# Attention sums spread one half a burst, turned two bursts later, with one bank wait per exp tile

## What is computed

```python
q, k = (x @ Wq) * scaling, x @ Wk          # 32 half-heads of 4 channels
v = x @ Wv                                  # 16 heads of 8 channels
probs = softmax(where(causal, q k^T, -inf))
attn = (probs[0::2] - lam * probs[1::2]) @ v
attn = attn * rsqrt(mean(attn^2) + eps) * rms_w * (1 - LAMBDA_INIT)
x = layernorm(x + attn @ Wo)
r, kk = sigmoid(xr @ W_r.T), square(relu(xk @ W_k.T))   # xr, xk mix x with the token before
x = layernorm(x + r * (kk @ W_v.T))
```

## Time and profile before

| | us |
|---|---|
| median of 3 runs | 507.17 (504.01 to 508.28) |
| profiled execution, device time | 505.25 |
| its span, first to last instruction | 503.5 |
| around the span | 1.75 |
| mean granted TensorE clock | 0.891 |

### The profile page before, as it was taken

How to read it: one execution, slowest core, us unless ns; L and a number is a source line. 1 busy time by engine, 2 the same in 40 slices (tenths; PEclk the granted TensorE clock), 3 DMA queues, 4 the chain that set the end, 5 groups by cost and what they waited for, 6 DMA issues and landing times.

```text
span 503.5 us, 14453 instructions
## 1 busy us (share of the span) xinstructions
PE 418.9 (83%) x5191; PEld 178.7 (35%) x5191; DVE 391.2 (78%) x504; ACT 354.7 (70%) x687; POOL 198.2 (39%) x349
## 2 busy tenths in 40 slices
PE   5665788898989898989898989889898978788682
PEld 3431323233434333333333333334242423344352
DVE  2769889797979999979797979898979894324633
ACT  3620168687878888968797969897969687756343
POOL 7000021253535364535354535545444445351512
PEclk9875569798979999979898979999989899989978
DMA  7695202011111120202020202020202010000001
GB/s 204 187 296 227 86 0 69 20 44 44 48 40 44 44 85 0 85 0 85 0 85 0 85 0 85 0 85 0 85 0 85 0 44 4 1 1 22 2 21 42
DMA packets 21082, 28.35 MB, mean 56 GB/s; under 512 B 3776, under 2 KB 8768, under 8 KB 21056
## 3 DMA queue, kind: packets, MB, share of 16 engines
q1 hardware_dynamic: 20624, 27.80, 17.5%
q10 hardware_dynamic: 432, 0.20, 0.2%
HBM read 18.29 MB, written 9.44 MB: 55 GB/s over the span
## 4 chain that ended last, share of the span: by engine, by line
PE 68%; ACT 15%; DVE 8%; issue 6%; DMA 1%; POOL 1%; ACTq 0%; POOLq 0%; DVEq 0%
PE acc L593 28%; PE ex L562 17%; ACT e_buf L898 11%; PE mx L516 7%; PE mx L508 6%; DVE part_max L989 5%; PE mx L690 1%; PE ex L624 1%; ACT o_tok L828 1%; PE ex L629 1%; PE mx L691 1%; DMA x_tok<-in_L_attn_x 1%; PE mx L675 1%; PE mx L710 1%; DVE rest L949 1%
## 5 line engine op out<-in xcount | busy, mean ns | idle before, releaser
L989 DVE TENSOR_REDUCE part_max<-mx 128x2 f32<-128x1024 f32 (+2 forms) x288 | 337.6, 1219 | 45.9 <-PE mx L508 35.8
L898 ACT ACTIVATE e_buf<-ex 128x512 f32<-128x512 f32 x576 | 312.1, 597 | 85.4 <-PE ex L562 81.0
L593 PE MATMUL acc<-e_buf,v_grp 128*32 128x256 f32 (+2 forms) x2200 | 185.5, 424 | 0.0
L562 PE MATMUL ex<-qe,ke 32*128 32x512 bf16 (+3 forms) x768 | 119.0, 346 | 44.0 <-ACT e_buf L898 29.2
L435 POOL TENSOR_SCALAR_AFFINE_SELECT e_buf<-e_buf 128x512 f32<-128x512 f32 x128 | 78.9, 634 | 169.5 <-ACT e_buf L898 169.4
L508 PE MATMUL mx<-km,qm 32*128 32x128 bf16 (+2 forms) x1280 | 124.4, 284 | 13.6 <-DVE part_max L989 12.1
L562 PEld LDWEIGHTS ex<-qe,ke 32*128 32x128 bf16 x768 | 30.9, 92 | 168.1 <-ACT e_buf L898 159.1
L593 PEld LDWEIGHTS acc<-e_buf,v_grp 128*32 128x32 f32 x2200 | 50.1, 115 | 65.6 <-issue 56.1
L508 PEld LDWEIGHTS mx<-km,qm 32*128 32x128 bf16 x1280 | 43.6, 96 | 25.9 <-DVE part_max L989 22.1
L516 PE MATMUL mx<-mask,pick 32*128 32x384 bf16 (+3 forms) x512 | 47.4, 308 | 0.0
L419 POOL TENSOR_TENSOR r_rms<-sq_eps,minus_half 128x16 f32<-128x16 f32 x15 | 43.7, 2910 | 1.2
(11 more groups left out here) (130 smaller groups left out, 266.3 us busy)
## 6 DMA issues: line engine op xcount, KB each, us to landing
qm<-q_rows SPq DMA_DIRECT2D x16, 256.0 KB, 2.7
km<-k_rows SPq DMA_DIRECT2D x16, 256.0 KB, 2.9
qe<-q_rows SPq DMA_DIRECT2D x16, 256.0 KB, 2.9
ke<-k_rows SPq DMA_DIRECT2D x16, 256.0 KB, 3.0
x_tok<-in_L_attn_x SPq DMA_DIRECT2D x2, 512.0 KB, 5.0
q_rows<-zero_rows SPq DMA_DIRECT2D x2, 512.0 KB, 5.8
k_rows<-ones_rows SPq DMA_DIRECT2D x2, 512.0 KB, 7.5
out<-v_all SPq DMA_DIRECT2D x4, 256.0 KB, 2.3
```

The source lines that it names most:

```text
L562: scored = pe.matmul(ex[:, ex_slot(b, i) % EX_BANKS, col:col + w], ke[par][rows, P * kb:P * (kb + 1)], qe[par][rows, q1 - w:q1], start=col ...
L593: last = pe.matmul(bank[STRIP * j:STRIP * (j + 1), hi - w:hi], v_grp[par][:, kb, j // 2, shift:shift + STRIP], e_buf[:, k % ESLOTS, j, col ...
L898: nc.scalar.activation(e_buf[:, k % ESLOTS, 2 * p + i, :], ex[:, ex_slot(b, i) % EX_BANKS, :], ACT.Exp).then_inc(s["exped"], 1)
L989: nc.vector.tensor_reduce(target, mx[m % 2][:].rearrange("p s (a b) -> p s a b", a=a), AX.X, ALU.max).then_inc(s["maxed"], 1)
```

## The change

Sum halves 0 and 1 move to burst 5, half 2 to burst 6, half 3 to burst 7; burst 4 alone has none. The sums are turned in burst 7 (it was 5), so the sums slot and the empty slot of the ring lie behind burst 7, and they are stored behind the exps of burst 7. The denominators are inverted in burst 10 (it was 8). `take_sums` is named in burst 4 and written ahead of that burst's exps; it was named in burst 3 and written behind that burst's. And in `score_pair` each of the two tiles waits for its own slot just ahead of its first matmul.

```diff
-TAKE_AT, TURN_AT, MAXIMA_AT, INVERT_AT = 3, 5, 13, 8
+TAKE_AT, TURN_AT, MAXIMA_AT, INVERT_AT = 4, 7, 13, 10
 LAG = 4
 SUMS_AT = {b: [(0, b - LAG)] for b in range(LAG, NB2)}
 SUMS_AT |= {b: [(1, NB2 - LAG + b)] for b in range(LAG)}
-SUMS_AT |= {4: [], 5: [], 6: [(0, 0), (0, 1)], 7: [(0, 2), (0, 3)]}
+SUMS_AT |= {4: [], 5: [(0, 0), (0, 1)]}
...
-                for i in range(2):
-                    place_free(n, ex_slot(b, i))
-                parts_here = QUADS[b // 2]
-                for c, kb, col, w in parts_here:
+                for c, kb, col, w in QUADS[b // 2]:
                     q1 = BANK * (c + 1)
                     for i in range(2):
+                        if col == 0:
+                            place_free(n, ex_slot(b, i))
                         j = 2 * (b % 2) + i
...
                     k, p = divmod(b, 2)
+                    if b == TAKE_AT and not (static and n == 0):
+                        take_sums(n - 1, 1 - par)
                     if p == 0:
                         wait(act, s["summed"], NQ * n + k - ESLOTS + 1)
...
-                    if b == TAKE_AT and not (static and n == 0):
-                        take_sums(n - 1, 1 - par)
```

## The result

The changed kernel takes 480.03 us (median of 4 runs, 475.44 to 482.79) against 507.73 (504.01 to 508.79): ratio 0.944, 95% interval 0.935 to 0.953. The forecast was 478, range 470 to 492. The profiled execution took 480.06, its span is 478.3, so 25.2 us less than the span before; the working had 29.6.

The account below looks back on a forecast made before the run. TensorE's chain, not full, was taken as the bound, with the half clock and full-clock groups above VectorE's 21.70 us to win; 22.5 in the loop plus 7.1 outside, 29.6 off 505.25, gave 475.7, by the median 478 us, range 470 to 492.

Parts of the forecast that it names:

- the ring: The PSUM banks that score tiles cycle through; a slot each was to gain 0.45 less 0.1 us in five bursts.
- Two prices, clock and group: Loop: the half clock costs 15.8 us; a full-clock group lies 1.5 us above VectorE's 21.70.
- Sums one half a burst, turn in burst 7: Bursts 5 to 8: moved sum halves and later turn take 4.52 us against 4.71, gain 0.19.
- The 1.94 through exps and store: Burst 7's scores to burst 8's second score tile: 1.94 us, the same as from burst 5 to 6 before.
- A slot for each tile: Score pairs: separate slot waits bring bursts 0, 1, 9, 14 and 15 from 1.07 to 0.98 us, 0.45 less 0.1.
- The inversion: Reciprocal moved from ahead of burst 9's reduction, 3.0 us later; a cost of 0.15 us a group was taken.
- The cover of 3.0 us: GpSimd's nine steps could end 3.0 us later before burst 0's sum needs quad 7's mask; the move uses it up.
- Taking the falls as gone: Loop: no group loses the clock any more, all 15.8 us gained; 12 x 22.6 = 271.2 against 293.7.
- its first sign: Granted clock 1.00 in the rows of all loop groups, with group times of 22.4 to 22.8 us.
- the stretch without sums: TensorE from burst 3's sums to the next sums: 4.19 us cut to about 2.3, too short for the clock to fall.
- Outside the loop: Groups 0, 1, 14 and 15: together 7.1 us gained, from clock and faster bursts; behind group 15 nothing changes.
- The slower case: Rival: two light stretches, at burst 4 and bursts 7 and 8, drop the clock in every group; 511 us, chance 0.06.

Follow-up runs that it names:

- e7: The changed kernel with burst 4's max unit scored three times over, same result, filling idle TensorE time; 473.3 us, ratio 0.933 to the kernel before.
- e8: The kernel before with burst 4's max unit scored four times and burst 5's twice, order untouched; 495.4 us, ratio 0.978.
- e1: The kernel before with only the slot waits of the change, one ahead of each tile's first matmul; 492.4 us, ratio 0.973.
- e12: The changed kernel with the denominators inverted in burst 12 in place of 10; 529.9 us, ratio 1.044 to the kernel before.
- e4: The kernel before with only the turned sums moved to burst 7 and the inversion to burst 10; 504.4 us, ratio 0.988.
- e2: The changed kernel with both slot waits of a pair ahead of its first matmul again, so the schedule alone; 486.0 us, ratio 0.957.
- e3: The kernel before with only the sum halves moved as in the change, the turn still in burst 5; 494.8 us, ratio 0.964.
- e15: The changed kernel with turn in burst 5, inversion in 8, burst 4's unit scored three times, group 15's sum halves as before; 470.4 us, ratio 0.927.
- e5: The changed kernel with the denominators inverted in burst 8 as before, in place of 10; 474.3 us, ratio 0.938 to the kernel before.

## Why the prediction was right, and where it was not

**Two prices, clock and group.** Right: of the loop's 18.2 us the clock gave 11.0 and the full-clock group 7.2. That the loop's groups take three times by the clock alone was in the rows by group, and e7 and e8 change the falls while the full-clock group stays.

**Sums one half a burst, turn in burst 7.** The working gave 4.52 from burst 5 to 8; 4.39 was measured. The 1.94 through exps and store is 1.86 in the changed kernel (186.76 to 188.62).

**A slot for each tile.** Right in sum (0.7 less 0.15 worked out, 0.60 measured) and nearly so by place: bursts 5 to 8 gain 0.34 for the 0.36 worked out, and the ring's bursts 0, 1, 9, 14 and 15 0.23 for the 0.45 less 0.1. Bursts 9 and 14 take 0.97 (0.98 was looked for), burst 1 1.03, and 0 and 15 stay at 1.09 and 1.08. Bursts 4, 16 and 17 gain 0.19 that was not forecast, and 2 and 10 lose 0.16, so part of the agreement is luck. By cause it was less clear: the slot waits alone (e1) are worth as much as the whole change, 0.23 of their 0.59 in bursts 5 to 8, where the working counted nothing for them. (Its round of exp, score and next exp adds up to 1.08, not 1.07, which changes nothing.)

**The inversion.** The cover of 3.0 us and its being used up were right; 0.15 was taken, 0.03 to 0.04 measured. It was worth its place among the rivals: e12.

**The clock.** The step that failed is "Taking the falls as gone": 15.8 us were to come back in the loop, 11.0 did. Three groups still fall, at 1.6 us each. Three was also the most that the prediction allowed before it called itself wrong, and its first sign, the clock at 1.00 in all loop groups, did not come. The reason given, that the clock follows the length of the stretch without sums, was too simple: with 2.2 us the clock still fell in group 4, behind the stretch and with the sums already running, and e4 with 3.5 us lost as much as the kernel before with 4.2. What stands is that light work at burst 4 is what drops it (e7, e8), and that the whole schedule keeps it better than either half (e2 against e3 and e4). Why some of the equal groups fall and others do not, and why most of e4's falls are cheaper, stays open, and so does how much the transposes weigh.

**Outside the loop.** 7.1 were worked out, 7.0 measured, by luck: groups 1 and 14 gave 2.3 more than thought, 2.0 came from the start, which the change does not touch, group 0 lost 0.4 where 0.5 were to be gained, and group 15 with the tail lost 2.0 where 1.5 were to be gained. In group 15 the clock is at half from 413 to 420 us of the span, over the sum halves and the feed-forward's first matmuls:

```profile
412.65 0.66 PE L681 MATMUL mx<-identf,x 128*128 128x128 f32 x4 [2.29 <-DVE x L1080]
...
415.12 1.93 PE L592 MATMUL acc<-e_buf,v_grp 128*32 128x256 f32 x16
416.99 2.08 PE L689 MATMUL mx<-x1T,w_cur 128*128 128x512 f32 x2
```

TensorE comes earlier to the turned `x1` and waits 2.29 us for it (1.68 before); the layer norm's chain over three engines is no faster. e15 puts 0.8 us of group 15 on the place of the halves. The 0.8 us of the tail are not the change's: e5 runs the same 130 matmuls there in 33.9 us with TensorE busy for 18.45, the change in 35.8 with it busy for 20.37. The rest is not settled.

**The rivals.** The slower case did not come. The Trainium skill, "TensorE: Matmul & The Clock Gate", section "A second HAM failure mode: psum-queue depth-cycling", names small idle times between groups of matmuls as enough to swing the clock. As a cause by themselves they find no support here: e7 keeps the ring and its waits and never falls in the loop.

## What to carry to other kernels

A repeated stage that takes several times is read by its rows with the granted clock first: what the clock costs and what the schedule costs are two sums, and the second can be had from the groups at full clock alone. Where a clock falls behind a light stretch, fill it with useful work, or test the cause with work that nobody needs, in time that is idle anyway. A step that is moved later has a last place at which it is free; work out its chain to the next one who waits, and look how near the new place is to it.

## What was not expected of the hardware

Extra matmuls made the kernel faster: 0.43 us of repeated scores a group are worth 480.0 to 473.3 us (e7), and 0.85 us 507 to 495 (e8). The clock can fall with no idle time of TensorE over 1 us: the longest ahead of the fall in group 6 of the kernel before is 0.98, in a stretch of 4.20 us that is busy for 2.17, and it can fall when dense work has just begun again (group 4 of the change). A stretch of 3.5 us (e4, 11 of 12 groups in one execution) kept it no better than one of 4.2 (before, 8 of 12). And equal groups of one execution differ, in a steady pattern.
